# Routing weights of the first experts fetched by transfers, and 32 of 68 weight parts of the second experts rounded in place

## The reference, cut to what matters

```python
x = x + set_attention(layernorm(x), ...)          # first layer
x = x + ffn0(layernorm(x), ...)                   # second layer: 16 experts of 96, top 4, and a shared expert
x = x + cross_attention(layernorm(x), ...)        # third layer
x = x + ffn1(layernorm(x), ...)                   # fourth layer: 8 experts of 704, top 2

def ffn0(x):                                      # the second layer
    scores = sigmoid(x @ router_w.T)
    _, topk_idx = top_k(scores + e_bias, 4)
    topk_w = take_along_axis(scores, topk_idx)
    topk_w = topk_w / (topk_w.sum(-1) + 1e-20)
    combine = zeros((T, 16)).at[arange(T)[:, None], topk_idx].add(topk_w)
    out = 0
    for e in range(16):
        g, u = split(x @ gate_up[e].T)
        out += combine[:, e:e + 1] * ((silu(g) * u) @ down[e].T)
    return out + shared(x)
```

## Time and profile before

| | us |
|---|---|
| median of 3 runs | 740.18 (740.11 to 740.99) |
| profiled execution, its own time | 740.54 |
| its span, from the first to the last instruction | 738.8 |
| busy: PE, PE weight load | 694.2, 622.9 |
| busy: DVE, POOL, ACT | 471.8, 356.1, 257.4 |

### The profile page before, as it was taken

One profiled execution on the slowest core, in us unless ns is written; L12 is line 12 of the kernel. 1 busy time (PEld: TensorE's weight loads), 2 busy tenths in 40 slices (PEclk: granted clock), 3 DMA queues, 4 the chain that ended last, 5 costly groups with the idle time before them and its releaser, 6 DMA issues.

```text
span 738.8 us, 14867 instructions
## 1 busy us (share of the span) xinstructions
PE 694.2 (94%) x4707; PEld 622.9 (84%) x4707; DVE 471.8 (64%) x1331; ACT 257.4 (35%) x484; POOL 356.1 (48%) x435
## 2 busy tenths in 40 slices
PE   4899999999999999998999984899999999999996
PEld 3758878888888888886677773799999999999995
DVE  4958597677777777775799958344544454454443
ACT  1355512333333333346466622222222232323221
POOL 6217693455446545549222034255354655465553
PEclk9786599999999999999899985899999999999999
DMA  9900103678877787769900047422425445434222
GB/s 220 343 3 1 58 0 122 236 247 271 264 242 257 262 265 248 248 230 430 367 20 31 31 138 267 147 44 41 154 45 151 97 122 155 151 75 135 44 37 22
DMA packets 60266, 114.96 MB, mean 156 GB/s; under 512 B 15185, under 2 KB 29394, under 8 KB 57778
## 3 DMA queue, kind: packets, MB, share of 16 engines
q1 hardware_dynamic: 50514, 103.48, 41.0%
q0 software_dynamic: 8736, 10.39, 8.5%
q10 hardware_dynamic: 960, 0.33, 0.2%
HBM read 68.89 MB, written 45.29 MB: 155 GB/s over the span
## 4 chain that ended last, share of the span: by engine, by line
PE 84%; DVE 10%; issue 3%; ACT 2%; DMA 1%; POOLq 0%; POOL 0%; DVEq 0%
PE ps L1114 19%; PE ps L1115 19%; PE ps L1116 19%; PE ps L1399 4%; PE ps L1244 2%; PE ps L1253 2%; PE ps L986 2%; PE ps L1290 2%; PE ps L1050 2%; PE ps L1041 2%; PE ps L1161 1%; PE ps L1266 1%; PE ps L1201 1%; PE ps L1378 1%; PE ps L1282 1%
## 5 line engine op out<-in xcount | busy, mean ns | idle before, releaser
L604 POOL TENSOR_TENSOR part_lo<-wexp,part_hi 128x256 fp32r<-128x256 f32 x136 | 104.8, 795 | 107.4 <-ACT part_hi L855 106.6
L715 POOL DMA_INDIRECT out_rows<-vbd,slot_row x39 | 63.3, 1623 | 105.6 <-DVE vbd L1947 74.0
L1114 PE MATMUL ps<-w_hi,x_high 128*128 x312 | 104.6, 335 | 1.1 <-DVE x_low L1952 1.1
L1115 PE MATMUL ps<-up_low,x_high 128*128 x312 | 101.1, 324 | 0.0
L1116 PE MATMUL ps<-w_hi,x_low 128*128 x312 | 101.0, 324 | 0.0
L1968 DVE TENSOR_TENSOR arena<-arena,ps 128x704 f32<-128x704 f32 x39 | 34.6, 888 | 102.5 <-ACT arena L954 102.5
L1114 PE MATMUL ps<-xn_high,gu_high 128*128 (+3 forms) x208 | 90.9, 437 | 0.0
L837 ACT ACTIVATE wexp<-ps 128x512 f32<-128x512 f32 (+1 forms) x52 | 31.1, 599 | 147.1 <-PE ps L1116 147.1
L1115 PE MATMUL ps<-xn_low,gu_high 128*128 (+3 forms) x208 | 81.9, 394 | 0.0
L1116 PE MATMUL ps<-xn_high,gu_low 128*128 (+3 forms) x208 | 81.7, 393 | 0.0
L954 ACT ACTIVATE arena<-ps 128x704 f32<-128x704 f32 x39 | 29.6, 760 | 119.1 <-PE ps L1116 119.1
(11 more groups left out here) (297 smaller groups left out, 1675.1 us busy)
## 6 DMA issues: line engine op xcount, KB each, us to landing
wexp<-in_wexp SPq DMA_DIRECT2D x68, 256.0 KB, 3.4
w_hi_rows<-part_hi SPq DMA_DIRECT2D x68, 256.0 KB, 3.1
w_lo_rows<-part_lo SPq DMA_DIRECT2D x68, 256.0 KB, 2.7
w_hi<-w_hi_rows SPq DMA_DIRECT2D x8, 2048.0 KB, 19.5
up_low<-w_lo_rows SPq DMA_DIRECT2D x8, 1408.0 KB, 6.0
down_low<-w_lo_rows SPq DMA_DIRECT2D x8, 768.0 KB, 8.3
wexp<-in_gu SPq DMA_DIRECT2D x2, 1632.0 KB, 11.2
xn_rows<-arena SPq DMA_DIRECT2D x8, 256.0 KB, 2.1
```

The lines of the kernel that those rows point to most:

```text
L604: r = pool.tensor_tensor(part_lo[:, n % 2, some], part_w[:, n % 4, some], part_hi[:, n % 2, some].bitcast(F32), ALU.subtract)
L715: pool.indirect_dma_start(out=out_rows, out_offset=bass.IndirectOffsetOnAxis(ap=slot_row[:, i:i + 1], axis=0), in_=yb[:, i % 2, :], in_off ...
L1114: pe.matmul(out, high, rows_high, start=start, stop=False, skip_group_check=True)
L1115: pe.matmul(out, high, rows_low, start=False, stop=False, skip_group_check=True)
```

## The change

The first experts' routing weights no longer come from a matmul. The chosen weights `cw0` of four tiles are turned in one fp32 transpose (`turn_weights`), copied by ACT to `cT` (fp32), stored by SP to a DRAM tensor `cw_rows` in four transfers (`store_weights`), and for each chunk two transfers read an expert's 512 weights with a repeat over its partitions into one of three buffers `w_spread` (`load_weights`: two chunks ahead of the next). DVE multiplies the up values in PSUM by them as soon as the up product is made, and the result by silu's output (both now in SBUF) after that. The first four tiles' transpose stands after `up0(0, 0)`, ahead of `up0(0, 1)`; ACT's copy of it ahead of the first silu.

Of the 68 parts, the 32 with an odd number within their 17 (two experts) are rounded by ACT into `part_whole` only for POOL's subtraction and not stored. The reload reads these columns from the weights given, the others from `w_hi_rows`, so that it goes in pieces of 512 columns. ACT rounds the 28 of experts 0 to 6 in place, two in each attention tile from tile 3 on, after a wait in tile 3 for the whole of `in_exp0`, and the 4 of expert 7 after the attention; PE waits for all 32. Some semaphores are merged (`q_centred`, `k_sum`, `k_spread`, `a_bias`), and the POOL instructions that made `spread` and a DVE memset go.

```diff
+        def is_stored(n):
+            return n % 17 % 2 == 0
+        LANDED0, LANDED7 = 16 * (4 * 2 + 3 * 4 + 2), 16 * (4 + 2)
@@ SP
+            def store_weights(first, groups):
+                for j in range(4):
+                    sp.dma_start(cw_v[:, first:first + groups, j, :],
+                                 cT[j * E0:(j + 1) * E0, first * P:(first + groups) * P].rearrange(
+                                     "e (g p) -> e g p", p=P)).then_inc(cw_stored, 16)
+            def load_weights(n):
+                g, c = n // (C0 - 1), chunk_of(n % (C0 - 1) + 1)
+                if n >= 3:
+                    sp.wait_ge(b_mult, n - 2)
+                sp.wait_ge(cw_stored, 16 * 8 if g else 16 * 4)
+                e = c * P // I0
+                edge = (e + 1) * I0 - c * P
+                for expert, lo, hi in ((e, 0, edge), (e + 1, edge, P)):
+                    sp.dma_start(w_spread[n % 3][lo:hi, :],
+                                 cw_rows[expert, g * 512:(g + 1) * 512].partition_broadcast(hi - lo)).then_inc(w_in[n % 3], 16)
...
+                if is_stored(n):
+                    sp.dma_start(w_hi_rows[:, part], high_of(n).bitcast(F32)).then_inc(hi_out[stored_ahead(n) % 2], 16)
...
+            sp.wait_ge(b_cT, 1)
+            store_weights(0, 1)
             sp.wait_ge(x_new, XA)
             for n in range(3):
                 load_part(n)
+            for n in range(3):
+                load_weights(n)
+            for g in range(NG):
+                for q in range(C0):
+                    if g == 0 and q == 10:
+                        sp.wait_ge(b_cT, 2)
+                        store_weights(1, NG - 1)
+                    for part in range(parts_by(g, q - 1), parts_by(g, q)):
+                        store_part(part)
+                    n = g * (C0 - 1) + q + 2
+                    if q and n < NG * (C0 - 1):
+                        load_weights(n)
...
+            def load_expert(e, landed):
+                at = e * WE
+                if e % 2 == 0:
+                    pairs = slice(at, at + 8 * PART)
+                    of = lambda rows: rows[:, pairs].rearrange("p (n two c) -> p n two c", two=2, c=PART)
+                    for half, src in enumerate((w_hi_rows, w_flat)):
+                        sp.dma_start(of(w_hi)[:, :, half, :].bitcast(F32), of(src)[:, :, half, :]).then_inc(landed, 16)
+                else:
...
             for e in range(7):
-                whole = slice(e * WE, (e + 1) * WE - D)
-                sp.dma_start(w_hi[:, whole].bitcast(F32), w_hi_rows[:, whole]).then_inc(in_exp0, 16)
+                load_expert(e, in_exp0)
@@ ACT
+            copy_weights(0, 1)
             def silu_group(g, k):
...
+            def round_part(n):
+                cols = slice(n * PART, (n + 1) * PART)
+                act.activation(w_hi[:, cols], w_hi[:, cols].bitcast(F32), ACT.Copy).then_inc(w_round, 1)
             for t in range(NT + 3):
+                early = ROUNDED[2 * (t - 3):2 * (t - 3) + 2] if 3 <= t < NT + 1 else []
+                if t == 3:
+                    act.wait_ge(in_exp0, LANDED0)
                 if 2 <= t < NT + 2:
                     copy_values(t - 2)
+                for n in early[0:1]:
+                    round_part(n)
                 if 1 <= t <= NT:
                     copy_probs(t - 1, t - 1)
+                for n in early[1:2]:
+                    round_part(n)
                 if t < NT:
                     exp_scores(t, t)
@@ PE
-                        pe.matmul(bank(4), spread[:, chunk_of(c) * P:(chunk_of(c) + 1) * P], cT[:, bass.ds(g * 512, 512)],
-                                  start=True, stop=True).then_inc(b_spread, 1)
...
             up0(0, 0, 0)
             pe.wait_ge(b_sig, 1)
+            pe.wait_ge(v_ready, B)
+            turn_weights(0)
             ffn0_group(0, 0)
@@ DVE
-                    dve.wait_ge(b_silu, i + 1)
-                    dve.tensor_tensor(hm0[0:rows_, c % 2, :], sg0[0:rows_, c % 2, :], bank(2 + c % 2)[0:rows_, :],
-                                      ALU.mult).then_inc(b_prod, 1)
+                    if c:
+                        dve.wait_ge(b_up, i + 1)
+                        dve.wait_ge(w_in[(c - 1) % 3], g * (32 * (C0 - 1) // 3) + 32 * ((c - 1) // 3 + 1))
+                        dve.tensor_tensor(hm0[:, c % 2, :], bank(2 + c % 2), w_spread[(c - 1) % 3], ALU.mult).then_inc(b_mult, 1)
+                        dve.wait_ge(b_mult, g * (C0 - 1) + c)
+                        dve.wait_ge(b_silu, i + 1)
+                        dve.tensor_tensor(hm0[:, c % 2, :], hm0[:, c % 2, :], sg0[:, c % 2, :], ALU.mult).then_inc(b_prod, 1)
...
-                    if c:
-                        dve.wait_ge(b_spread, g * (C0 - 1) + c)
-                        dve.tensor_tensor(hm0[:, c % 2, :], hm0[:, c % 2, :], bank(4), ALU.mult).then_inc(b_mult, 1)
-                        dve.wait_ge(b_mult, g * (C0 - 1) + c)
```

More of the change, by code:

```diff
@@ L355, in program @@
         NG = NT // 4
-        weights5 = bank(5).bitcast(BF16)
-        WEIGHTS_AT = [bank(4).bitcast(BF16)[:, 0:512], weights5[:, 0:512], weights5[:, 512:1024], weights5[:, 0:512]]
+        w_spread = [view(wexp, at, 512) for at in (20416, 20928, 4096)]
+        w_in, cw_stored = [sem(f"w_in{n}") for n in range(3)], sem("cw_stored")
+        cw_rows = nc.dram_tensor("cw_rows", (E0, NT * P), F32, kind="Internal").ap()
         PIECE = 256
@@ L365, in parts_by, with stored_ahead, high_of @@
             return PARTS0 + (g - 1) * PARTS + (c + 1) * PARTS // C0
+        def is_stored(n):
+            return n % 17 % 2 == 0
+        def stored_ahead(n):
+            return n - n // 17 * 8 - n % 17 // 2
+        def high_of(n):
+            return part_hi[:, stored_ahead(n) % 2, :] if is_stored(n) else part_whole
+        LANDED0, LANDED7 = 16 * (4 * 2 + 3 * 4 + 2), 16 * (4 + 2)
+        w_round = sem("w_round")
+        NSTORED = stored_ahead(NPART)
+        ROUNDED = [n for n in range(NPART) if not is_stored(n)]
+        ROUNDED7 = [n for n in ROUNDED if n * PART >= last]
         def chunk_rows(q):
@@ new lines, in _ @@
+            sp.wait_ge(x_new, XA)
+            for n in range(3):
+                load_part(n)
+            for n in range(3):
+                load_weights(n)
[9 more added lines that the diff above has]
+                        load_weights(n)
@@ L465, in _ @@
             sp.wait_ge(x_new, XC)
-            sp.dma_start(w_hi[:, last:last + WE - D].bitcast(F32), w_hi_rows[:, last:last + WE - D]).then_inc(in_exp7, 16)
+            load_expert(7, in_exp7)
             load_tails(7, 1, in_exp7)
@@ L1003, in _ @@
             pe.wait_ge(a_routed, 2)
-            pe.matmul(bank(7)[:, 0:NK], ones[0:1, :], brow, start=True, stop=True).then_inc(a_bias, 1)
+            pe.matmul(bank(7)[:, 0:NK], ones[0:1, :], brow, start=True, stop=True).then_inc(a_route, 1)
             def score_sets(b):
@@ L1218, in _ @@
             pe.wait_ge(in_bo, 16)
-            pe.wait_ge(b_mult, NG * (C0 - 1))
+            pe.wait_ge(b_cT, 2)
             for k in range(KD):
```

171 lines of the change are left out of this document (68 added, 103 removed).

## The result

The change made the kernel slower: 759.91 us, median of 4 runs (756.69 to 760.78), beside 740.14 for the kernel before in 4 runs on the same chip (732.08 to 740.99). The ratio is 1.0284, 95% interval 1.0206 to 1.0362. The forecast was 748.2, its range 739.5 to 757.0: the sign was right, the size less than half of what was measured. The profiled execution took 760.39 us with a span of 758.6, which is 19.8 above the span of before. Executions of one kernel spread by 1 to 2%, the longer ones at a lower mean granted clock (before on one chip: 731.9 us at 0.969, 740.8 at 0.953), and the profiled executions of the experiments 1, 8 and 9 are among the slow ones of their kernels, so traces are compared by stage and not by their totals.

The account below looks back on a forecast made before the run. PE was taken to bound the second layer. Second layer −7.7, wait +12.7, work done in it −0.7, clock +1.7 and rounding +2.0 made +8.0: 748.5 beside 740.54, 748.2 beside the median, range 739.5 to 757.0.

Parts of the forecast that it names:

- The wait at tile 3: Attention tile 3: ACT, there at 354.9, waits 12.7 us for the reload landing at 367.6; work done meanwhile returns 0.7.
- The routing matmul: Second layer: each matmul removed saves 0.24 us of PE, −8.6 in groups 1 to 3 and −2.2 in group 0.
- The start of group 0: Second layer's beginning: a new chain of stores and fetches brings weights at 100.8; a lateness of 3.1 us is carried on.
- The reload: Reload of experts 0 to 6 in 2 KB rows: 382 GB/s in place of 430, 38.4 us, +4.3.
- The clock less what the stop gave back: Attention after the wait: a spell of lower clock costs +1.7, and work done in the wait gives back 0.7.
- the rounding in the tiles: Attention: 28 roundings by ACT cost only in the 6 tiles with `scale_rows` before them, +2.0, bounds 0 and 4.
- Transfers in the second layer: Second layer: the DMA share becomes 0.86, fetches and loads go out ahead of use, nothing is late, cost nothing.
- the term of 2.9 us a group: Second layer: DVE's second multiplication takes 0.93, 2.9 us more a group, 46.7 of 55.7, covered by PE, cost nothing.
- The reload's start: End of the second layer: the reload starts with the last down product, 7.7 earlier, at 321.4.
- The working by the Trainium skill, SBUF: Second layer: DVE's second multiplications all held by GpSimd, 50.4 us of DVE a group, the sum 3 higher.
- slow reload: Rival on the reload: 329 GB/s, a wait of 18.9, sum +14.2, 754.4 us; chance 0.19.
- second layer not faster: Rival on the second layer: DVE or transfers eat the gain, 0 for 7.7, sum +15.7, 755.9 us; chance 0.14.

Follow-up runs that it names:

- experiments 1: The change with ACT's wait for the reload moved from attention tile 3 to tile 8, ten roundings behind the attention: 736.13 us, ratio 0.9962.
- eighth run: The change with the wait at tile 8, without the 36 stores of high parts and 45 of the 48 weight fetches: 736.04 us, ratio 0.9969.
- 9: The change with the wait at tile 8 and SP's weight fetch put ahead of a chunk's part transfers: 736.26 us, ratio 0.9965.
- the fifth experiment: The kernel before with only ACT's wait at tile 3 for the reload added: 748.41 us, ratio 1.0152.
- the seventh experiment: The change with the wait at tile 8, the 36 stores of high parts left out, all parts reloaded from the input: 734.75 us, ratio 0.9956.
- sixth: The change with its wait at tile 3 kept and the 32 roundings in place left out: 753.59 us, ratio 1.0239.
- the third experiment: The kernel before, with its routing matmuls, plus the change's stores, reload, wait at tile 3 and roundings: 756.65 us, ratio 1.0240.
- the eleventh: The kernel before, with its routing matmuls, plus half of the high parts rounded in place in ACT's idle stretches behind the attention tiles: 736.33 us, ratio 0.9991.
- seven traces named behind the eleventh experiment: Traces of all kernels with both fetched weights and roundings in place, the change included: 304.3 to 305.2 us from the attention's output to the end.
- the six others: Traces of the kernels without both fetched weights and roundings in place: 301.5 to 303.6 us from the attention's output to the end.

## Why the prediction was off

*Right.* The wait at tile 3 is the cost, and the fifth experiment shows it with its predicted price (10.2 measured by the medians, 10.5 in the trace; a wait of 8.4 plus 1.0 was expected). The routing matmul is worth what was read from the earlier trace rows where nothing else holds: five chunks in a row stand 4.18 us apart (silu at 232.28, 236.46, 240.64, 244.82, 249.00) where before has 4.41. The start of group 0: DVE could begin at 100.97, for 100.8, and PE's down matmul at 104.35, for 104.5. That the group ended 0.9 late, for 3.1 − 2.2, is in part luck: 0.7 of it was there at the group's first silu (93.66 for 93.00). The reload ran at 385 GB/s, for 382, and took +4.7 for +4.3. By the Trainium skill, DMA: Bandwidth & Descriptors, Measured, whose 341 GB/s is for transfers of 1 MB issued from GpSimd, it would have been an estimate of +8.9; the trace bears out the row-based value, SP's transfers of 1 MB and less, back to back, running at 385. The clock less what the stop gave back cost 0.8 to 1.5, for 1.0, and the rounding in the tiles 1.9 to 2.9, for 2.0 with a bound of 4.

*Wrong.* The step that failed is "Transfers in the second layer": the share was right at 0.86, and the conclusion "nothing is late", "Cost nothing", was not. Its cover was counted in issue time and in buffers of loads and fetches, and the third user of buffers, POOL's two for low parts, was left out, as was the growth of every landing. A second reading failed with it: the reload was moved with the last down product, one of two conditions that coincided in before. Since ACT stands until the data land, the landing decides. It was forecast for 367.6 and came at 376.7, 9.1 late: 5.2 because the second layer gained 2.5 and not 7.7, 3.4 because the reload started behind the last store and no longer with the last down product, and 0.5 from its own length with ACT's restart. With 0.7 in the tiles and 2.0 at the end that makes the 11.8 between +8.0 and +19.8. In detail:

- The second layer. Some 2 to 3 us of the missing 5.2 are the queue's (the seventh experiment against the change and the first and sixth). Most of the rest is the term of 2.9 us a group: an undisturbed group gained 2.0, with less load on the queue than the change has (seventh and eighth). So the conclusion "Cost nothing" on DVE's two multiplications was wrong too, by about 0.9 a group, 2.7 in all, and the eighth run's rows show PE waiting for DVE at both places where most of it is lost.
- The reload's start. I had moved it with the last down product, 329.1 − 7.7 = 321.4; in the change it hangs on the last part's store. From the layer's end to the reload it took 3.1 us before, 6.5 in the change, and 3.6 with the high stores left out. It started at 330.0, 8.6 later than forecast.
- The wait. ACT came at 357.6, for 354.9 (5.2 of the gain missing, 2.5 given by the absent spell of low clock), and the data at 376.7, for 367.6: 12.7 − 2.7 + 9.1 = 19.1, the idle time of the row. The spell of low clock changed the wait's length and not the time, since ACT waited anyway.

The working by the Trainium skill, SBUF — State Buffer, Who interferes with whom, had an estimate of about 1 us a group for DVE in the chunks that also add and take statistics. That is what the eighth run left (0.9), and in that run's trace the chunk behind the statistics is where PE waits; but the estimate took every second multiplication as held, and in the change their median was 0.69 and their mean 0.80. DVE's lines in the change (busy us, mean ns, idle):

```profile
L1751 DVE TENSOR_TENSOR wexp<-wexp 128x512 f32<-128x512 f32 x48 | 38.3, 797 | 1.6
L1760 DVE CAST h_high<-wexp 128x512 fp32r<-128x512 f32 x48 | 33.7, 702 | 1.6
```

The second multiplication took 0.80 for my 0.93 and ranged from 0.69 to 1.27, near the two values forecast. The cast behind it, which wasn't touched, went from 0.51 in the same stretch of before to 0.70. DVE's group is 48.0 us busy for my 46.7.

In the rivals I had kept "slow reload" and "second layer not faster" apart, as alternatives. They don't exclude each other: the first lengthens the wait and the second delays everything ahead of it. Added together, +6.2 and +7.7 on my +8.0, they would have reached 21.9, and the range would have held the result. It would have been right by luck in part, since the reload wasn't slow but late. The last term, +2.0 from the attention's output to the end, I didn't forecast; 1.5 of it lies between the last two scattering additions, at the low clock shown above, and its cause is open. "A measurement of this kernel can tell 0.2%" was wrong as well: the 95% intervals here are 0.6 to 0.8% to either side with 4 runs and 0.4 to 0.5% with 10.

## What to carry to other kernels

When a wait is put into a loop, set its place by when the data land in the changed kernel, and move it as late as its users allow: here five tiles took away an idle time of 19.1 us. Read the queue's share not only as a capacity: ask which buffers are held until a landing, and what a longer landing does to each of them. When a transfer is said to "start earlier", look at all the conditions that it waits for before moving it with one of them: two that come true together in the kernel before can part in the changed one. Where an engine stands in a wait, count the time from what ends the wait. And two rivals that don't exclude each other can both come true: price them together.

## What was not expected of the hardware

With the share of the DMA engines going from 0.77 to 0.86 in group 1, the median landing of the same 256 KB transfers grew by 34 to 56% (2.7 to 4.2, 3.5 to 4.7, 3.3 to 5.0 us); with 0.76 in the seventh run, in which smaller fetches share the queue, it was 3.0 and 4.1 over the layer.

The spell of low clock at 350 to 358 is in the traces of before and of the third experiment (granted clock 0.69 and 0.50 from 350 to 354 and from 354 to 358) and not in those of the change and of the eleventh (1.00 and 1.00). The third and the eleventh run the same instructions up to tile 3 and ended their second layers at the same 325.90; ACT came to tile 3 at 362.6 and at 359.9. So such a spell of the lower of the two levels (1.2 and 2.4 GHz) is in one execution and not in the other, and a difference of one profiled pair below 3 us that spans such a place should not be read as the change's.

After the stop of 19 us PE ran at 1.2 GHz for most of the next 8 us (granted clock 0.55 from 377 to 385), but the fifth and sixth runs put no more than 0.8 to 1.5 on the clock, less what the stop gave back. My reading is that PE had tile 3's front part done by then; no run tried it.

The last block of the kernel ran most or all of its down matmuls at the lower level (0.21 to 0.22 us apart) in the seven traces named behind the eleventh experiment, and at the upper (0.12 apart) in the six others. In the change and in before PE had stood idle for the same 2.0 us ahead of them. Between the change and before this was worth 1.5 us.
